# Layer 1 of an adapter and feed-forward kernel: the middle tap of the convolution added by accumulating DMAs

## The chip, the cores and the metric

The kernel runs on 1 core of one Trainium2 chip. The metric is device time in microseconds, the median of several runs. The engines are PE (TensorE, matrix multiplies and transposes), DVE (VectorE), ACT (ScalarE), POOL (GpSimd) and SP (SyncE, which here issues DMAs only).

## The reference

`x` is 8 batches of 512 tokens of 256 numbers. Two layers are applied, each `x = x + ffn(cond(x))`. Layer 0 is an adapter with a layer norm, and a feed-forward block with ternary weights and activations quantized per token. Layer 1, the one that is changed:

```python
def _L1_ffn_ref(x, w1, conv_w, conv_b, w2):
    h = bit_linear(x, w1)                       # 256 -> 1024, ternary weights
    h = depthwise_conv1d(h.transpose(0, 2, 1), conv_w, conv_b)   # 3 taps along the 512 tokens, padding 1
    h = h.transpose(0, 2, 1)
    h = jax.nn.silu(h)
    return bit_linear(h, w2)                    # 1024 -> 256
```

`bit_linear` quantizes each token's row by its largest absolute value to 8 bits.

## The kernel before, in words

All is one program with instruction lists written out by hand for each engine. Each engine runs its list in order; semaphores hold it where it needs another's result. The lists are: an opening, a loop `slot1` over batches of layer 0, a closing in which both layers overlap, and a loop `slot2` over rounds `s` of layer 1. In a round, several batches stand in the pipeline at once: `x` and the linear layer of batch `s`, the first product and the convolution of batch `s-1`, the silu and second product of batches `s-2` and `s-3`.

The 1024 hidden channels of a batch lie as 8 blocks `f` of 128 partitions with 512 tokens along each. For each block:

- PE makes the product into a PSUM bank (`up`, L1337), and DVE dequantizes it into `apad` (`dequant`, L1018);
- ACT writes the last tap into the bank (`last_tap`, L608), and DVE adds the first tap to it and writes `conv[b % 2]`, which is half of `raw_all` (`first_tap`, L1025, it counts up `p_first`);
- POOL writes the middle tap and the bias into `mid` (`middle_tap`, L805, it counts up `p_mid`). For every two blocks, a quarter `q` of the batch, POOL adds `mid` onto `conv` (`tap_sum`, L812, 128 x 1024 f32, it counts up `p_sum`). There are two `mid` buffers, so `middle_tap` waits for the sum two quarters back.

When all four quarters are there, PE transposes them, 128 tokens `k` at a time (`transpose_conv(b, k)`, L1350). ACT applies silu (L617) into one of two buffers `g2`. DVE takes the largest absolute value of each token (`absmax2`, L1031), and then a scale and its reciprocal; ACT rounds to 16-bit codes (`round2`, L627); SP issues a DMA transpose (`transpose2`, L399), and PE multiplies by the second weights (`down2`, L1365). DVE adds the result to `x` (`final2`, L1049), and SP stores it (L403). Of the same round are `load2` on SP (L389, 256 KB of weights of the linear layer), `spread_of_up` (L790) and `round_y` (L784) on POOL, and `scale_of_down` (L795) on POOL.

PE's order in a round puts `transpose_conv(s-2, 0)` after `up(s-1, 4)`; ACT's puts `silu(s-2, 0)` between the last taps of blocks 3 and 4; DVE's puts `absmax2(s-2, 0)` before `first_tap(s-1, 4)`.

Of the kernel before, what the change touches and what calls it, by code (L numbers as in the profile page):

```python
# [6 lines left out]
ALU = mybir.AluOpType  # L7
# [4 lines left out]
BF16 = mybir.dt.bfloat16  # L12
# [3 lines left out]
P = 128  # L16
# [12 lines left out]
def build_program(nc, t):  # L29
    B, S, D = t["x"].shape  # L30
    H = t["w1a"].shape[1]
# [5 lines left out]
    TB = S // P  # L37
# [4 lines left out]
    with ExitStack() as ctx:  # L42
        def sb(name, shape, dt=F32):
            return ctx.enter_context(nc.sbuf_tensor(name, shape, dt))

        def sem(name):
            return ctx.enter_context(nc.semaphore(name))

        def sems(name, n):
            return [sem(f"{name}{k}") for k in range(n)]  # L50

        def wait(eng, s, n):

            if isinstance(n, int) and n <= 0:
                return
            eng.wait_ge(s, n)
# [3 lines left out]
        def bank(k, n=1):  # L60
            return psum[:, k, :] if n == 1 else psum[:, k:k + n, :]
# [25 lines left out]
        taps = sb("taps", [P, KH, 3])  # L87
# [13 lines left out]
        gam = [sb(f"gam{k}", [P, D]) for k in range(2)]  # L101
        bet = [sb(f"bet{k}", [P, D]) for k in range(2)]
        dqb = [sb(f"dqb{k}", [P, S]) for k in range(2)]
        mid_all = [sb(f"mid{k}", [P, 2 * S + 1]) for k in range(2)]
        hT = sb("hT", [A + 1, S])
        xx = [sb("xx", [P, 2, D]), dqb[0][:, :].rearrange("p (a d) -> p a d", a=2)]

# [28 lines left out]

        xs = sb("xs", [P, PAIRS, 2, D])

        lowb = mid_all[0][:, 0:H].bitcast(BF16)
        junk = mid_all[1][:, 0:H].bitcast(BF16)  # L140
        BANK_AD, BANK_DN, BANK_QT, BANK_UP, BANK_IN = 0, 1, 2, 3, 7

        BANK_TOTAL = [BANK_UP + 3, BANK_UP + 3, BANK_IN, BANK_IN]
# [77 lines left out]
        apad = sb("apad", [P, KH, SP2])  # L221
# [6 lines left out]
        qs2 = [sb(f"qs2_{k}", [P, 1]) for k in range(2)]  # L228
        dq2 = [sb(f"dq2_{k}", [P, 1]) for k in range(TB)]

        mid = [mid_all[k][:, 1:2 * S + 1].rearrange("p (r s) -> p r s", r=2) for k in range(2)]
        BANK_C, BANK_D2 = 5, 1


# [32 lines left out]
        p_last = sem("p_last")  # L267
        p_mid = sem("p_mid")
        p_first = sem("p_first")
        p_sum = sem("p_sum")  # L270
        p_cT = sems("p_cT", TB)
        p_silu = sems("p_silu", TB)
        p_am2 = sem("p_am2")
# [29 lines left out]
        def tile(b, j):  # L303
            return TB * b + j + 1
# [373 lines left out]
        def _(pool):  # L678
# [119 lines left out]
            def middle_tap(b, f):  # L798
                pool.wait_ge(p_a, KH * b + f + 1)
                if b == 0:  # L800
                    pool.wait_ge(s_const, 32)
                    pool.wait_ge(s_tern[3], 1)
                    pool.wait_ge(s_wsum, 4)
                wait(pool, p_sum, TB * b + f // 2 - 1)
                pool.tensor_scalar(mid[f // 2 % 2][:, f % 2, :], apad[:, f, 1:S + 1], taps[:, f, 1:2],  # L805
                                   convb[:, f:f + 1], ALU.mult, ALU.add).then_inc(p_mid, 1)

            def tap_sum(b, q):
                c = conv[b % 2]
                pool.wait_ge(p_first, KH * b + 2 * q + 2)  # L810
                pool.wait_ge(p_mid, KH * b + 2 * q + 2)
                pool.tensor_tensor(c[:, 2 * q:2 * q + 2, :], c[:, 2 * q:2 * q + 2, :],  # L812
                                   mid[q % 2][:, :, :], ALU.add).then_inc(p_sum, 1)

            def round2(b, k):
                pool.wait_ge(p_qs2[k], b + 1)
# [28 lines left out]
            def slot2(s):  # L845
                on(middle_tap, s - 1, 0)
                on(middle_tap, s - 1, 1)
                on(middle_tap, s - 1, 2)
                on(scale_of_down, s - 3, 1)
                on(scale_of_down, s - 3, 2)  # L850
                on(tap_sum, s - 1, 0)
                on(middle_tap, s - 1, 3)
                on(scale_of_down, s - 3, 3)
                on(middle_tap, s - 1, 4)
                on(tap_sum, s - 1, 1)
                on(spread_of_up, s)
                on(round_y, s, 1)
                on(round_y, s, 0)
                on(scale_of_down, s - 2, 0)
                on(middle_tap, s - 1, 5)  # L860
                on(middle_tap, s - 1, 6)
                on(middle_tap, s - 1, 7)
                on(tap_sum, s - 1, 2)
                on(tap_sum, s - 1, 3)
# [293 lines left out]
        def _(pe):  # L1158
# [181 lines left out]

            def transpose_conv(b, k):
                if k == 0:
                    pe.wait_ge(p_sum, TB * b + TB)
                    if b == 0:
                        pe.wait_ge(s_gelu, tile(B - 1, TB - 1))
                    wait(pe, p_silu[TB - 1], b)
                else:
                    pe.wait_ge(p_silu[k - 1], b + 1)
                for f in range(KH):
                    ins = pe.transpose(bank(BANK_C + f // KT)[:, (f % KT) * P:(f % KT + 1) * P],  # L1350
                                       conv[b % 2][:, f, k * P:(k + 1) * P], id32[:, :])
                ins.then_inc(p_cT[k], 1)
# [16 lines left out]
            def slot2(s):  # L1369
                on(transpose_conv, s - 3, 3)  # L1370
                on(transpose_x, s, 0)
                on(up, s - 1, 0)
                on(up, s - 1, 1)
                on(up, s - 1, 2)
                on(down2, s - 3, 0)
                on(linear, s, 0)
                on(transpose_x, s, 1)
                on(up, s - 1, 3)
                on(up, s - 1, 4)
                on(transpose_conv, s - 2, 0)  # L1380
                on(linear, s, 1)
                on(down2, s - 3, 1)
                on(transpose_conv, s - 2, 1)
                on(up, s - 1, 5)
                on(up, s - 1, 6)
                on(up, s - 1, 7)
                on(down2, s - 3, 2)
                on(transpose_conv, s - 2, 2)
                on(spread_scales, s)
                on(transpose_y, s)  # L1390
                on(down2, s - 3, 3)
# [67 lines left out]
```

## Time and profile before

| | us |
|---|---|
| median of 3 runs | 321.74 |
| lowest and highest | 318.56, 323.08 |
| span of the profiled execution | 319.6 |

The profiled execution is one run of the program; its span reaches from the first to the last instruction, and no other time of that execution is given. Busy shares of it: DVE 87%, PE 83%, POOL 81%, ACT 75%. Layer 0 fills the first 140 us or so, layer 1 the time from about 160 us on. Busy times of one engine can overlap a little where one instruction starts before the one in front has ended, so a group's mean is slightly longer than its share of the engine's time.

### The profile page before, as it was taken

The page shows a single profiled execution, that of the slowest core. Times are in us where ns is not written, and L with a number is a line of the kernel's source. Part 1 is how long each engine was busy: PE and PEld are TensorE (multiplying, and loading weights), DVE is VectorE, ACT ScalarE, POOL GpSimd, SP SyncE. Part 2 cuts the span into 40 slices and gives each one's busy share as a digit, 9 for nine tenths or more (in the row PEclk, how much of TensorE's full clock was granted, in tenths as well). Part 3 has the DMA queues.
Part 4 walks back from the last instruction along what each step waited for, and adds up shares of the span by engine and source line. Part 5 has one row for each costly group of instructions (what it writes and reads, how often), then busy time and mean ns, then how long its engine had stood idle before and what let it go on. Part 6 is the DMA issues. An engine that isn't in the chain of part 4 may idle for free. (4 is left out here: it accounts for less than half of the span.)

```text
span 319.6 us, 6460 instructions
## 1 busy us (share of the span) xinstructions
PE 264.5 (83%) x1676; PEld 179.7 (56%) x1700; DVE 276.6 (87%) x606; ACT 240.6 (75%) x366; POOL 259.2 (81%) x402
## 2 busy tenths in 40 slices
PE   6679878869798887999889797989899898967574
PEld 6234334535455454566656665868587686745452
DVE  0778988896899989955899999999999999999671
ACT  4588897966776487567566888889989888978770
POOL 2567899996898988759999999998989799898310
PEclk9977799999999999999999999999999999999997
DMA  7995773579496368454430333445436373444764
GB/s 249 320 363 118 222 197 76 113 159 213 100 215 126 75 87 178 69 100 91 44 66 2 60 74 66 118 98 91 111 93 122 70 98 82 101 98 100 120 145 115
DMA packets 90745, 39.50 MB, mean 124 GB/s; under 512 B 73005, under 2 KB 88141, under 8 KB 90710
## 3 DMA queue, kind: packets, MB, share of 16 engines
q1 hardware_dynamic: 84532, 30.47, 46.8%
q10 hardware_dynamic: 6178, 8.62, 8.6%
q8 instruction: 14, 0.23, 0.3%
q14 instruction: 21, 0.17, 0.2%
HBM read 18.11 MB, written 4.19 MB: 70 GB/s over the span
## 5 line engine op out<-in xcount | busy, mean ns | idle before, releaser
L812 POOL TENSOR_TENSOR raw_all<-raw_all,mid 128x1024 f32<-128x1024 f32 x32 | 63.7, 2000 | 0.7 <-DVE raw_all L1025 0.7
L548 ACT ACTIVATE g<-banks,dqz 128x1024 f32<-128x1024 f32 x32 | 35.5, 1112 | 24.4 <-POOL r L757 21.2
L805 POOL TENSOR_SCALAR mid<-apad,taps,convb 128x512 f32<-128x512 f32 x64 | 48.8, 774 | 0.5 <-DVE apad L1018 0.5
L608 ACT ACTIVATE banks<-apad,taps 128x512 f32<-128x512 f32 x64 | 42.3, 682 | 6.9 <-DVE apad L1018 6.8
L970 DVE TENSOR_REDUCE am<-g 128x1 f32<-128x1024 f32 x32 | 38.6, 1211 | 8.6 <-ACT g L548 8.5
L1025 DVE SCALAR_TENSOR_TENSOR raw_all<-apad,taps,banks 128x512 f32<-128x512 f32 x64 | 45.8, 743 | 0.0
L1018 DVE TENSOR_TENSOR apad<-banks,dqb 128x512 f32<-128x512 f32 x64 | 40.9, 684 | 4.6 <-PE banks L1337 4.5
L757 POOL TENSOR_SCALAR r<-g,qs 128x1024 uint16<-128x1024 f32 x32 | 36.8, 1153 | 6.2 <-DVE qs L982 5.9
L1365 PE MATMUL banks<-tern,q1T 128*128 128x256 bf16 x256 | 33.8, 276 | 9.5 <-DMA q1T<-r 8.0
L1227 PE MATMUL banks<-tern,qT 128*128 128x512 bf16 x117 | 36.6, 388 | 5.5 <-ACT qcT L540 3.3
L627 ACT ACTIVATE r<-g,qs 128x1024 uint16<-128x1024 f32 x32 | 36.6, 1144 | 5.3 <-DVE qs L1044 3.2
L1298 PE MATMUL banks<-wl,x2T 128*128 128x256 f32 x128 | 33.0, 387 | 8.8 <-ACT x2T L577 6.8
L1031 DVE TENSOR_REDUCE am<-g 128x1 f32<-128x1024 f32 x32 | 38.8, 1213 | 1.2 <-ACT g L617 1.2
L1241 PE MATMUL banks<-tern,q1T 128*128 128x256 bf16 x256 | 33.2, 272 | 5.7 <-DVE xs L989 4.1
L1350 PE MATMUL banks<-id,raw_all 128*128 128x128 f32 x256 | 33.5, 274 | 3.6 <-ACT g L617 2.5
L617 ACT ACTIVATE g<-banks 128x1024 f32<-128x1024 f32 x32 | 32.5, 1014 | 4.0 <-PE banks L1350 3.7
L1365 PEld LDWEIGHTS banks<-tern,q1T 128*128 128x128 f16 x256 | 23.8, 98 | 18.5 <-DMA q1T<-r 12.5
L1337 PE MATMUL banks<-yT,tern 128*128 128x512 bf16 x115 | 29.7, 379 | 3.9 <-DVE raw_all L1025 2.4
L1241 PEld LDWEIGHTS banks<-tern,q1T 128*128 128x128 f16 x256 | 24.1, 97 | 15.7 <-issue 6.7
L1350 PEld LDWEIGHTS banks<-id,raw_all 128*128 128x128 f32 x256 | 28.9, 141 | 7.1 <-ACT g L617 3.9
L1298 PEld LDWEIGHTS banks<-wl,x2T 128*128 128x128 f32 x128 | 21.8, 190 | 15.1 <-issue 11.2
L1228 PE MATMUL banks<-bias9b,qcT 128*128 128x512 bf16 x64 | 24.8, 387 | 0.0
(116 smaller groups left out, 561.5 us busy)
## 6 DMA issues: line engine op xcount, KB each, us to landing
out_y<-xs SPq DMA_DIRECT2D x32, 128.0 KB, 2.0
xs<-in_x ACTq DMA_DIRECT2D x7, 512.0 KB, 5.7
x2T<-in_xT ACTq DMA_DIRECT2D x4, 512.0 KB, 5.2
wl<-in_cwl SPq DMA_DIRECT2D x8, 256.0 KB, 2.7
xT<-in_xT ACTq DMA_DIRECT2D x3, 512.0 KB, 4.2
raw_all<-in_w1a ACTq DMA_DIRECT2D x1, 1024.0 KB, 5.0
cw<-in_cw SPq DMA_DIRECT2D x16, 64.0 KB, 5.0
gam<-in_gamma SPq DMA_DIRECT2D x8, 128.0 KB, 3.0
```

The lines of the kernel that those rows point to most:

```text
L608: act.activation(bank(BANK_U[g % 3]), apad[:, f, 2:S + 2], ACT.Copy, scale=taps[:, f, 2:3]).then_inc(p_last, 1)
L757: pool.tensor_scalar(r1[j][:, :], g1[j % 2][:, :], qs1[j % 2][:, 0:1], CODE, ALU.mult, ALU.add) \
L805: pool.tensor_scalar(mid[f // 2 % 2][:, f % 2, :], apad[:, f, 1:S + 1], taps[:, f, 1:2], convb[:, f:f + 1], ALU.mult, ALU.add).then_inc(p_ ...
L812: pool.tensor_tensor(c[:, 2 * q:2 * q + 2, :], c[:, 2 * q:2 * q + 2, :], mid[q % 2][:, :, :], ALU.add).then_inc(p_sum, 1)
L970: dve.tensor_reduce(am1[j % 2][:, :], g1[j % 2][:, :], AX_X, ALU.max, apply_absolute_value=True) \
L1018: dve.tensor_tensor(apad[:, f, 1:S + 1], bank(BANK_U[(KH * b + f) % 3]), dqb[b % 2][:, :], ALU.mult) \
L1025: dve.scalar_tensor_tensor(out=conv[b % 2][:, f, :], in0=apad[:, f, 0:S], scalar=taps[:, f, 0:1], in1=bank(BANK_U[(KH * b + f) % 3]), op0= ...
L1031: dve.tensor_reduce(am2[k % 2][:, :], g2[k % 2][:, :], AX_X, ALU.max, apply_absolute_value=True) \
L1241: pe.matmul(o, q1T[j][:, c, :].bitcast(F16), w_dn0[:, c, :], start=(c == 0), stop=False)
L1298: pe.matmul(bank(bank_y(b))[:, a * D:(a + 1) * D], x2T[:, 2 * k + a, j, :], wl1[par][:, j, :], start=(j == 0), stop=False)
L1350: ins = pe.transpose(bank(BANK_C + f // KT)[:, (f % KT) * P:(f % KT + 1) * P], conv[b % 2][:, f, k * P:(k + 1) * P], id32[:, :])
L1365: pe.matmul(o, q2T[k % 2][:, f, :].bitcast(F16), w_dn1[:, f, :], start=(f == 0), stop=False)
```

## The change

POOL's addition becomes a DMA that POOL issues: it reads `mid[q]` and adds it in the destination, `conv`. There are four `mid` buffers, one for each quarter, and four semaphores in place of one, which count 16 for each DMA. The buffers are no longer shifted by one element. The two scratch tiles `lowb` and `junk` of the opening lie in the new buffers.

```diff
-        mid_all = [sb(f"mid{k}", [P, 2 * S + 1]) for k in range(2)]
+        mid = [sb(f"mid{k}", [P, 2, S]) for k in range(TB)]
...
-        mid = [mid_all[k][:, 1:2 * S + 1].rearrange("p (r s) -> p r s", r=2) for k in range(2)]
...
-        p_sum = sem("p_sum")
+        p_sum = sems("p_sum", TB)
...
-                wait(pool, p_sum, TB * b + f // 2 - 1)
-                pool.tensor_scalar(mid[f // 2 % 2][:, f % 2, :], apad[:, f, 1:S + 1], taps[:, f, 1:2],
+                wait(pool, p_sum[f // 2], 16 * b)
+                pool.tensor_scalar(mid[f // 2][:, f % 2, :], apad[:, f, 1:S + 1], taps[:, f, 1:2],
                                    convb[:, f:f + 1], ALU.mult, ALU.add).then_inc(p_mid, 1)
...
             def tap_sum(b, q):
                 c = conv[b % 2]
                 pool.wait_ge(p_first, KH * b + 2 * q + 2)
                 pool.wait_ge(p_mid, KH * b + 2 * q + 2)
-                pool.tensor_tensor(c[:, 2 * q:2 * q + 2, :], c[:, 2 * q:2 * q + 2, :],
-                                   mid[q % 2][:, :, :], ALU.add).then_inc(p_sum, 1)
+                pool.dma_start(c[:, 2 * q:2 * q + 2, :].rearrange("p r s -> p (r s)"),
+                               mid[q][:, :, :].rearrange("p r s -> p (r s)"), accum_op=ALU.add) \
+                    .then_inc(p_sum[q], 16)
...
             def transpose_conv(b, k):
                 if k == 0:
-                    pe.wait_ge(p_sum, TB * b + TB)
+                    for q in range(TB):
+                        pe.wait_ge(p_sum[q], 16 * (b + 1))
```

The order of the lists stays. On POOL, in a round of the loop, the end of one batch and the start of the next stand like this before, with the semaphores that each waits for:

```order
L805 TENSOR_SCALAR mid<-apad,taps,convb 128x512 [waits p_sum,p_a] x3
L812 TENSOR_TENSOR raw_all<-raw_all,mid 128x1024 [waits p_mid,p_first] x2
L805 TENSOR_SCALAR mid<-apad,taps,convb 128x512 [waits p_sum,p_a] x3
L795 TENSOR_SCALAR dq_1<-s_1,ws 128x1 [waits p_s2,p_o1]
L795 TENSOR_SCALAR dq_2<-s_0,ws 128x1 [waits p_s2,p_o2]
```

And on POOL now, in the same place:

```order
L804 TENSOR_SCALAR mid<-apad,taps,convb 128x512 [waits p_sum2,p_a]
L804 TENSOR_SCALAR mid<-apad,taps,convb 128x512 [waits p_sum3,p_a] x2
L811 DMA raw_all<-mid 128x1024 [waits p_mid,p_first] x2
L804 TENSOR_SCALAR mid<-apad,taps,convb 128x512 [waits p_sum0,p_a] x2
L804 TENSOR_SCALAR mid<-apad,taps,convb 128x512 [waits p_sum1,p_a]
```

The additions of quarters 2 and 3 have become two DMAs in their place, and each middle tap waits for the DMA of its own quarter of the batch before.

## Rows read from the trace of the kernel before

**Rows 1.** The page: its first line, busy times, and busy tenths in 40 slices.

```profile
span 319.6 us, 6460 instructions
PE 264.5 (83%) x1676; PEld 179.7 (56%) x1700; DVE 276.6 (87%) x606; ACT 240.6 (75%) x366; POOL 259.2 (81%) x402
...
DVE  0778988896899989955899999999999999999671
```

**Rows 2.** Windows, three rounds: busy us of each engine, PEclk, DMA share, GB/s.

```profile
229.20:247.60 18.40, 16.74 (x124) 13.28 (x125) 18.32 (x36) 16.58 (x23) 16.87 (x22) 1.00 0.51 101
247.60:266.10 18.50, 17.05 (x126) 13.52 (x127) 18.39 (x36) 16.46 (x23) 16.72 (x22) 1.00 0.51 87
266.10:284.50 18.40, 14.51 (x108) 11.08 (x109) 18.32 (x36) 15.97 (x22) 17.29 (x24) 1.00 0.39 86
```

**Rows 3.** Waits, 157 to 300 us: us in total, times, longest.

```profile
POOL dqy L790 <- DVE sy L1006: 5.3, 7, 1.2
...
DVE apad L1018 <- PE banks L1337: 1.2, 3, 0.7
...
DVE xs L989 <- PE banks L1242: 0.3, 1, 0.3
...
DVE am L1031 <- ACT g L617: 0.2, 1, 0.2
```

**Rows 4.** Groups by line, 157 to 300 us: busy us, mean ns, idle before.

```profile
L812 POOL TENSOR_TENSOR raw_all<-raw_all,mid 128x1024 f32<-128x1024 f32 x32 | 63.7, 2000 | 0.7 <-DVE raw_all L1025 0.7
L805 POOL TENSOR_SCALAR mid<-apad,taps,convb 128x512 f32<-128x512 f32 x62 | 47.3, 774 | 0.5 <-DVE apad L1018 0.5
L1025 DVE SCALAR_TENSOR_TENSOR raw_all<-apad,taps,banks 128x512 f32<-128x512 f32 x64 | 45.8, 743 | 0.0
...
L1018 DVE TENSOR_TENSOR apad<-banks,dqb 128x512 f32<-128x512 f32 x61 | 38.9, 684 | 1.4 <-PE banks L1337 1.2
L1031 DVE TENSOR_REDUCE am<-g 128x1 f32<-128x1024 f32 x28 | 34.0, 1213 | 0.2 <-ACT g L617 0.2
```

**Rows 5.** Timeline of POOL in one round: start us, us, instruction, idle before.

```profile
236.06 0.27 POOL L790 TENSOR_SCALAR dqy<-sy,ws 128x4 f32<-128x4 f32 x1 [1.25 <-DVE sy L1006]
...
240.93 3.96 POOL L812 TENSOR_TENSOR raw_all<-raw_all,mid 128x1024 f32<-128x1024 f32 x2
```

**Rows 6.** Timelines of DVE, PE and ACT in the same round.

```profile
241.26 0.75 DVE L1025 SCALAR_TENSOR_TENSOR raw_all<-apad,taps,banks 128x512 f32<-128x512 f32 x1
...
250.83 1.21 DVE L1031 TENSOR_REDUCE am<-g 128x1 f32<-128x1024 f32 x1
...
247.56 1.04 PE L1350 MATMUL banks<-id,raw_all 128*128 128x128 f32 x8
...
255.00 1.04 PE L1365 MATMUL banks<-tern,q1T 128*128 128x256 bf16 x8
...
257.74 1.04 PE L1365 MATMUL banks<-tern,q1T 128*128 128x256 bf16 x8
...
249.54 1.01 ACT L617 ACTIVATE g<-banks 128x1024 f32<-128x1024 f32 x1
```

**Rows 7.** Timeline of SP's queue in the same round; the us are the issue's.

```profile
242.37 0.41 SPq L389 DMA_DIRECT2D wl<-in_cwl  x1
243.60 1.25 SPq L399 DMA_TRANSPOSE q1T<-r  x1
244.90 0.57 SPq L403 DMA_DIRECT2D out_y<-xs  x1
248.09 1.25 SPq L399 DMA_TRANSPOSE q1T<-r  x1
...
253.72 1.23 SPq L399 DMA_TRANSPOSE q1T<-r  x1
```

**Rows 8.** DMA: rates in 40 slices of 242.3:245.5, of 247.8:251.8; landing, 157 to 300.

```profile
GB/s 301 282 288 241 20 6 0 0 0 0 0 0 0 0 102 205 205 115 26 38 77 166 346 397 384 358 320 256 218 64 0 74 195 224 214 237 202 224 202 202
...
GB/s 0 0 0 0 0 0 0 0 0 0 0 0 0 0 26 156 225 215 205 230 202 202 220 212 202 182 202 331 374 369 287 92 0 0 0 0 0 0 0 0
...
q1T<-r SPq DMA_TRANSPOSE x29, 3.1
```

**Rows 9.** Timeline of the tail, 295 to 304 us.

```profile
295.78 2.00 POOL L812 TENSOR_TENSOR raw_all<-raw_all,mid 128x1024 f32<-128x1024 f32 x1 [0.71 <-DVE raw_all L1025]
...
297.83 1.09 PE L1350 MATMUL banks<-id,raw_all 128*128 128x128 f32 x8 [0.45 <-POOL raw_all L812]
...
298.96 1.02 ACT L617 ACTIVATE g<-banks 128x1024 f32<-128x1024 f32 x1 [0.17 <-PE banks L1350]
...
299.31 1.05 PE L1365 MATMUL banks<-tern,q1T 128*128 128x256 bf16 x8 [0.39 <-DMA q1T<-r]
...
300.01 1.22 DVE L1031 TENSOR_REDUCE am<-g 128x1 f32<-128x1024 f32 x1 [0.65 <-ACT g L617]
...
303.32 1.15 ACT L627 ACTIVATE r<-g,qs 128x1024 uint16<-128x1024 f32 x1 [0.92 <-DMA q1T<-r]
```

More of the change, by code:

```diff
@@ L137, in build_program @@
         xs = sb("xs", [P, PAIRS, 2, D])
-        lowb = mid_all[0][:, 0:H].bitcast(BF16)
-        junk = mid_all[1][:, 0:H].bitcast(BF16)
+        lowb = mid[0][:, :, :].rearrange("p r s -> p (r s)").bitcast(BF16)
+        junk = mid[1][:, :, :].rearrange("p r s -> p (r s)").bitcast(BF16)
         BANK_AD, BANK_DN, BANK_QT, BANK_UP, BANK_IN = 0, 1, 2, 3, 7
```

## The prediction

> **What bounds the kernel now.** I read the page first [rows 1]: DVE is busy 87% of the span, PE 83%, POOL 81%, and the tenths show DVE at 9 without a gap from the 23rd slice to the 37th, which is the second layer. The run shown in these rows has a span of 319.6 us; the median of the runs is 321.74 (318.56 to 323.08), so my sum is made against 319.6 and carried to the median by adding the same microseconds. Then the stretches [rows 2]: three successive rounds of the layer-1 loop, one batch each, take 18.4, 18.5 and 18.4 us (36 DVE instructions in each), and in each DVE is busy for 18.3 to 18.4 of them, POOL for 16.7 to 17.3. The DMA engines are about half used. So a round lasts as long as DVE's list of instructions; POOL has 1.1 to 1.8 us to spare per round. The waits from 157 to 300 us [rows 3] say the same from the other side: DVE's waits are 1.2 + 0.3 + 0.2 = 1.7 us in 143, while POOL waits for DVE (5.3 us). What POOL does is therefore not what a round's length is made of, provided that nobody gets POOL's product late.
>
> **What is removed.** Each `tap_sum` is one POOL addition of 2.00 us [rows 4], 32 in all, four per round, 8.0 us of POOL's round. They are replaced by 32 DMAs. Four `mid` buffers in place of two add no wait: a buffer is wanted again a round later, and a DMA that takes under 18 us is long over. The writes into `mid` now start at an even place; between 774 ns a piece for 512 columns [rows 4] and no change I cost this at nothing, since it lies in POOL's slack.
>
> The gain from POOL's freed time is small. DVE can only gain the 1.7 us that it waits [rows 3], and most of that is for matmuls; I take 0.5 us, bounds 0 and 1.7. The free time also does not start the following work earlier, because POOL's next item after the second sum waits for DVE's scale already (1.25 us idle at 236.06) [rows 5].
>
> **What the issue costs.** POOL spends something to issue a DMA; no row of before has one from POOL. The nearest are SP's, 0.57 us for a plain store and 1.25 us for a transpose [rows 7]. I take 1.0, ends 0.3 and 2.5. Up to 2.0 + 1.7/4 = 2.4 us per DMA it stays within POOL's own slack.
>
> **Where the product is wanted.** PE transposes the sum (`transpose_conv(b,0)`), and waits for all four quarters of batch b. In a steady round: DVE ends the last first tap, `first_tap(b,7)`, at 241.26 + 0.75 = 242.0 [rows 6]; POOL has ended both last sums at 240.93 + 3.96 = 244.9 [rows 5]; PE starts the transposes at 247.56 for 1.04 us; ACT's silu (1.01 us) starts at 249.54; DVE's `absmax2(b,0)` starts at 250.83 [rows 6]. In the tail, where nothing else stands between them, the three hand-overs take 0.03 to 0.05 us each [rows 9]. So the sum may land as late as 250.83 - 0.03 - 1.01 - 0.04 - 1.04 - 0.05 = 248.7 before DVE stands still; today there is 3.8 us in hand. Between 242.0 and 250.83 DVE works through its own list, so this allowance of 6.7 us from the last first tap is the same each round and does not grow when a round is longer. Any excess is paid in full by DVE, once per round.
>
> **How late the DMA lands.** Quarter 2 is issued when the last middle tap ends, 240.93 [rows 5]; a transpose issued at 248.09 has its first packets at about 249.3 [rows 7, 8], so quarter 2's data begins at about 242.0. Quarter 3 is issued from 242.0 on. In the same stretch the engines must carry SP's other transfers [rows 7]: the linear weights (issued 242.37), a transpose (243.60), a store (244.90). Prices: 256 KB of weights at the 397 GB/s seen in that stretch, 0.7; a 256 KB transpose at about 205 GB/s [rows 8], 1.3; a 128 KB store 0.4. The accumulating transfer of 512 KB is not in the trace. Lower end: a copy at the best rate seen, 0.524 MB at 397 GB/s, 1.3 us. Upper end: each byte of the sum is read from two places, both at the transpose's rate, 4.9 us. I take the rate of the nearest row, the transpose, which also reads and writes this core's memory: 0.524 MB at 205 to 215 GB/s, 2.5 us. From 242.0: 2.5 + 2.5 + 0.7 + 1.3 + 0.4 = 7.4, and 0.2 to the semaphore: 249.6, against 248.7 allowed. **Stall 0.9 to 1.0 us per round.** At 1.3 us each it would be 247.2, no stall; at 4.9 it would be 254.4, 5.7 per round.
>
> Of the other transfers, the transposes feed `down2`. The one issued at 248.09 shares the engines with quarter 0 (issued near 247.6) and can be 2.5 us late; its matmuls start at 255.00 [rows 6], some 3.8 after it landed. Quarter 1 follows `first_tap(b,3)`, near 251, and is over by 255; the transpose of 253.72, whose matmuls start at 257.74 [rows 6], lands after 3.1 us [rows 8], has about 0.9 us in hand and only grazes it. These I cost at nothing; with longer transfers they are the next to be late.
>
> The Trainium skill (page "DMA: Bandwidth & Descriptors", section "Anatomy of one DMA — SWDGE (gpsimd) path") gives a transfer issued from POOL about 2.0 us plus its bytes at 436 GB/s, an estimate of 3.2 us here; by it quarter 3 would land at 245.2 and the stall term of the sum would be 0. No row of before tests it, and it speaks of copies on idle engines. Its page "Collectives: The Full Stack" (section "The bandwidth ceiling: the fold count and why AG ≠ RS ≠ AR") says that a DMA that adds needs two source reads and delivers half as fast, about 31/2 GB/s per engine, an estimate of 2.1 us of data on 16 engines; by that the stall would be 0.1 to 0.2 us. That rule speaks against the change, though less than the row I took.
>
> **The tail.** Batch 7's last sum starts at 295.78 and ends at 297.78; PE's transposes wait for exactly that (0.45) [rows 9]. The DMA issued then has data at 296.9, shares with one transpose and lands near 300.7, 2.9 us later. `down2(6,1)` stands behind it on PE and goes from 299.31 to 301.8, and with it the transpose that waits for its bank; but the chain there already waits for other transposes, and `round2(7,0)` had 0.92 us of waiting for one [rows 9]. About half gets through: +1.5, ends 0 and 3.
>
> **Sum.** Rounds with batches 1 to 6 in them: 6 x 1.0 = 6.0; tail 1.5; POOL's relief -0.5: **+7.0 us**, 319.6 to 326.6 for the span, 321.7 to about **329** for the median.
>
> **The rivals.**
> 1. *Forecast, 0.48*: PE gets the sum up to 2 us late per round. Stall 0.4 to 2.0, so +3.5 to +14: 325 to 336.
> 2. *All hidden, 0.33*. The addition lands inside the 6.7 us allowed: transfers of 1.3 to 2.2 us. For it: 3.8 us in hand today, engines half idle [rows 2]. Against: the other transfers fall into just this stretch. It is also where the skill's first rule would lead. Stall 0, tail 0 to 3, relief 0.5: -1 to +3, 321 to 325. This ends on the other side of the forecast: not slower. It decides at a transfer of 2.0 us with my queue.
> 3. *The DMA engines become the bound, 0.13*. They are busy 0.51 x 18.4 = 9.4 us a round [rows 2]; four transfers of 4.9 add 19.6, together 29.0 against 18.4, +10.6 a round, +64 over six: 386; at 3.5 each 23.4, +5, 352. It decides above (18.4 - 9.4)/4 = 2.25 us each, so my own 2.5 stands at its edge. The same picture results if POOL's issue costs over 2.4 us.
> 4. *Faster by 2%, 0.06*. POOL's additions slow DVE's two-operand instructions. The first tap takes 743 ns, the dequantizing product 684 for the same columns [rows 4]; if the difference were POOL's doing, 64 x 0.06 = 3.8, with the 1.7 of waits 5.5: 316. Against: the medians do not spread.
>
> **How the numbers follow.** This kernel's runs spread 1.4%, and 2%, 6.4 us, is about what can be told from no change. Above 328.2 lie 0.29 of the forecast's 0.48 and all 0.13 of the third: slower 0.42. Within: 0.19 and the 0.33 of the second: 0.52. Faster 0.06. The range goes from 319 (below the hidden case) to 345 (a transfer of about 3 us); outside are most of the third case and the fourth.
>
> **What would show it.** DVE gets a wait before `absmax2` for ACT's silu, of about 1 us per round, with PE's first transposes waiting for a DMA; POOL's busy time falls by 63.7 us less what issuing shows; DVE's means of 684, 743 and 1213 ns stay; the DMA share of a round rises from 0.51 to 0.9 or more; rounds of 19.4 us. Wrong if the sum lands less than 6.7 us after the last first tap (then case 2), or if the SP transposes, 3.1 us today [rows 8], take over 5 and `final2` waits for matmuls too (case 3).

## The result, and the profile after

The change made the kernel slower: the median of 4 runs is 346.06 us (341.95 to 348.21), that of before beside them 321.59 (318.56 to 323.08). The ratio is 1.0738, 95% interval 1.0625 to 1.0852. Forecast were 329 us and a range that ended at 345. Here and below a median is that of all runs, and a ratio is that of the fast ones alone, without those that lie over 1.5% above a kernel's fastest (here 348.21), so it can differ a little from the quotient of the medians. The profiled execution has a span of 343.3 us, 23.7 more than before's 319.6.

The page after: its first lines, and the tenths of DVE and of the DMA engines.

```profile
span 343.3 us, 6468 instructions
...
PE 278.5 (81%) x1676; PEld 190.3 (55%) x1700; DVE 275.0 (80%) x606; ACT 240.9 (70%) x366; POOL 222.8 (65%) x402
...
DVE  0668987998899899659979879696997999976361
...
DMA  7992674867774574464997979989999998999864
```

DVE is as busy as before in microseconds (275.0 against 276.6), but its row of nines [rows 1] is broken from the middle on, and there the DMA row is nearly all nines. Windows of three rounds, from one `absmax_y` (L1000) to the next, and of the tail behind the last of them; the columns are those of [rows 2]:

```profile
200.92:222.70 21.78, 18.30 (x125) 14.60 (x125) 18.33 (x36) 16.53 (x23) 12.41 (x21) 0.92 0.95 175
...
222.70:244.61 21.91, 18.30 (x125) 14.30 (x126) 18.44 (x36) 16.81 (x23) 12.41 (x21) 0.92 0.99 176
244.61:264.89 20.28, 17.17 (x123) 13.17 (x124) 18.42 (x37) 16.62 (x23) 12.42 (x21) 1.00 1.05 183
...
285.33:343.30 57.97, 39.82 (x249) 30.05 (x249) 37.40 (x75) 33.07 (x37) 18.56 (x34) 0.82 0.87 156
```

A round lasts 20.3 to 21.9 us in place of 18.4, with DVE still busy for 18.4: it now stands still for 1.9 to 3.5 us in each. POOL is down from 16.8 to 12.4. The DMA share has gone from 0.51 to about 1. PE's granted clock was 0.92 in the first two of these rounds, and they lost more (2.8 and 3.4 us) than the two at 1.00 behind them (2.0 each). By the starts of L1000, the round that ends at 200.92 is 3.8 us longer than before's, the next ones 2.8, 3.4, 2.0 and 2.0, and the tail is 58.0 against 48.4: 14.0 us in the rounds, 9.5 in the tail, nothing ahead of them.

The waits of 157 to 325 us (us in total, times, longest), the two groups of POOL, and the DMA queues (packets, MB, share of 16 engines) of the same stretch:

```profile
ACT g L616 <- PE banks L1351: 17.6, 14, 4.2
...
DVE am L1031 <- ACT g L616: 13.5, 7, 4.4
...
PE banks L1351 <- DMA raw_all<-mid: 13.0, 6, 3.3
PE banks L1366 <- DMA q1T<-r: 11.4, 6, 3.4
```

```profile
L804 POOL TENSOR_SCALAR mid<-apad,taps,convb 128x512 f32<-128x512 f32 x62 | 47.8, 806 | 21.8 <-DVE apad L1018 21.8
L811 POOL DMA_DIRECT2D raw_all<-mid x32 | 27.6, 867 | 10.3 <-DVE raw_all L1025 9.7 <-POOL mid L804 0.2
```

```profile
q0 software_dynamic: 4608, 16.78, 55.7%
q1 hardware_dynamic: 35584, 12.20, 43.6%
```

Two kinds of wait have appeared side by side: PE for the sum (`raw_all<-mid`), which goes on to ACT and DVE, and PE for SP's transposes (`q1T<-r`). Before, DVE's wait for ACT's silu was 0.2 us [rows 3]. The adding DMAs are q0: 55.7% of 168 us, 93.6 us for 32, so **2.93 us of all 16 engines each**. From issue to landing they take 6.9 us in the median (4.5 at the least), the transposes 6.2 in place of 3.1 [rows 8].

One round as timelines of POOL, DVE, PE, ACT and DVE again (start us, us, instruction, idle before):

```profile
251.10 0.78 POOL L811 DMA_DIRECT2D raw_all<-mid  x1
252.52 0.85 POOL L811 DMA_DIRECT2D raw_all<-mid  x1 [0.65 <-DVE raw_all L1025]
...
251.47 0.75 DVE L1025 SCALAR_TENSOR_TENSOR raw_all<-apad,taps,banks 128x512 f32<-128x512 f32 x1
...
255.39 1.05 PE L1366 MATMUL banks<-tern,q1T 128*128 128x256 bf16 x8 [1.95 <-DMA q1T<-r]
...
260.62 1.06 PE L1351 MATMUL banks<-id,raw_all 128*128 128x128 f32 x8 [0.50 <-DMA raw_all<-mid]
...
261.72 1.02 ACT L616 ACTIVATE g<-banks 128x1024 f32<-128x1024 f32 x1 [0.58 <-PE banks L1351]
...
259.73 1.29 DVE L1018 TENSOR_TENSOR apad<-banks,dqb 128x512 f32<-128x512 f32 x2 [1.23 <-PE banks L1337]
...
262.78 1.22 DVE L1031 TENSOR_REDUCE am<-g 128x1 f32<-128x1024 f32 x1 [0.32 <-ACT g L616]
```

The last first tap ends at 252.22, quarter 3's DMA is issued at 252.52, and PE starts on the sum at 260.62: 8.4 us behind the first tap, where 6.7 to landing was allowed. PE also stood 1.95 us for a transpose at 255.39; what it does behind that is late, and DVE waits 1.23 us for an `up` product. So in this round DVE stands longer by way of the late transpose than by way of the late sum (0.32 us).

The chain of waits in the first of the windows above shows sum and clock together (start us, us, what):

```profile
208.85 8.55 DMA raw_all<-mid
...
217.64 1.94 PE banks L1351 x8
```

The 8 transposes of PE behind the sum took 1.94 us in place of 1.06. PE had stood 3.29 us for the sum, and its granted clock was 1.2 GHz (0.5) from 217.1 to 220.5 us.

### The profile page after: what moved, and what is told of

Read it like the earlier page. It is cut to its first block, busy times and chain, and to the rows that moved or that the text cites. A ratio compares the mean times of both kernels' runs of the same rounds, so it can differ in the third digit from the quotient of the medians.

```text
span 343.3 us, 6468 instructions
## 1 busy us (share of the span) xinstructions
PE 278.5 (81%) x1676; PEld 190.3 (55%) x1700; DVE 275.0 (80%) x606; ACT 240.9 (70%) x366; POOL 222.8 (65%) x402
## 4 chain that ended last, share of the span: by engine, by line
DMA 24%; PE 21%; issue 18%; POOL 18%; DVE 10%; ACT 4%; SPq 3%; POOLq 0%; DVEq 0%; ACTq 0%
DMA q1T<-r 10%; DMA raw_all<-mid 10%; PE banks L1298 6%; POOL r L756 4%; PE banks L1366 3%; PE banks L1351 3%; POOL mid L804 3%; POOL xs L729 2%; DMA cw<-in_cw 2%; PE banks L1241 2%; PE banks L1227 2%; ACT r L626 2%; DMA bet<-in_beta 1%; SPq L334 1%; DVE zg L939 1%
## 5 line engine op out<-in xcount | busy, mean ns | idle before, releaser
L1366 PE MATMUL banks<-tern,q1T 128*128 128x256 bf16 x256 | 37.7, 297 | 15.2 <-DMA q1T<-r 14.6
L1351 PE MATMUL banks<-id,raw_all 128*128 128x128 f32 x256 | 38.8, 302 | 13.6 <-DMA raw_all<-mid 13.0
L1351 PEld LDWEIGHTS banks<-id,raw_all 128*128 128x128 f32 x256 | 33.2, 157 | 18.3 <-issue 15.6
L756 POOL TENSOR_SCALAR r<-g,qs 128x1024 uint16<-128x1024 f32 x32 | 37.5, 1174 | 6.8 <-DVE qs L982 6.5
L1366 PEld LDWEIGHTS banks<-tern,q1T 128*128 128x128 f16 x256 | 26.0, 106 | 25.7 <-DMA q1T<-r 18.6
L1298 PE MATMUL banks<-wl,x2T 128*128 128x256 f32 x128 | 35.7, 411 | 4.1 <-issue 3.8
L1241 PE MATMUL banks<-tern,q1T 128*128 128x256 bf16 x256 | 33.2, 272 | 6.6 <-DVE xs L989 6.0
L811 POOL DMA_DIRECT2D raw_all<-mid x32 | 27.6, 867 | 10.3 <-DVE raw_all L1025 9.7
L1241 PEld LDWEIGHTS banks<-tern,q1T 128*128 128x128 f16 x256 | 24.2, 97 | 15.9 <-issue 9.2
L1298 PEld LDWEIGHTS banks<-wl,x2T 128*128 128x128 f32 x128 | 23.6, 205 | 11.4 <-issue 7.3
L1049 DVE SCALAR_TENSOR_TENSOR xs<-banks,dq,xs 128x256 f32<-128x256 f32 x32 | 15.4, 481 | 11.8 <-PE banks L1367 11.7
```

Of the source, the lines that this page charges most:

```text
L756: pool.tensor_scalar(r1[j][:, :], g1[j % 2][:, :], qs1[j % 2][:, 0:1], CODE, ALU.mult, ALU.add) \
L1241: pe.matmul(o, q1T[j][:, c, :].bitcast(F16), w_dn0[:, c, :], start=(c == 0), stop=False)
L1298: pe.matmul(bank(bank_y(b))[:, a * D:(a + 1) * D], x2T[:, 2 * k + a, j, :], wl1[par][:, j, :], start=(j == 0), stop=False)
L1366: pe.matmul(o, q2T[k % 2][:, f, :].bitcast(F16), w_dn1[:, f, :], start=(f == 0), stop=False)
```

## The experiments

All ratios are to the kernel before, on the same chip; the brackets hold the 95% interval. S stands for the theory that the sum lands too late, T for the one that traffic makes SP's transposes late.

**The traffic without the wait for the sum.**

```diff
-                pool.dma_start(conv quarter q, mid[q], accum_op=ALU.add).then_inc(p_sum[q], 16)
+                pool.dma_start(mid[q], conv quarter q, accum_op=ALU.add).then_inc(p_sum[q], 16)
...
-                    for q in range(TB): pe.wait_ge(p_sum[q], 16 * (b + 1))
+                    pe.wait_ge(p_first, KH * (b + 1))
```

> The same 32 accumulating DMAs of 512 KB, issued by POOL at the same places, but in the other direction: conv is added onto mid, which nobody reads, and PE's first transpose waits for the first taps alone. The middle tap and the bias are left out of the result. Theory S (the time goes because PE waits for the sum, which lands 7 to 8 us after its issue): the waits before transpose_conv and silu go, 320 to 325 us. Theory T (the DMA engines are full, four transfers of 2.9 us and 9 us of others in a round of 18.4, and SP's transposes get late with everything behind them): nothing is gained by not waiting for the sum, 338 to 346 us, q1T still landing after about 6 us. Both in part: 326 to 337.

Measured 341.5 us, 1.0679 [1.0576, 1.0782]. Waits, 157 to 325 us:

```profile
PE banks L1365 <- DMA q1T<-r: 18.5, 10, 3.6
...
DVE xs L1049 <- PE banks L1366: 11.5, 8, 2.8
```

With no wait for a sum anywhere, 21 us of the loss are there, and PE's waits are for the transposes. "Transposes at nothing" is refuted.

**Two quarters by DMA, two by POOL**: first 2 and 3, then 0 and 1. The edit is the same in all kernels that mix (`BY_DMA` is the set):

```diff
+                if q in BY_DMA:
                     pool.dma_start(...)
+                else:
+                    pool.tensor_tensor(c[:, 2 * q:2 * q + 2, :], c[:, 2 * q:2 * q + 2, :],
+                                       mid[q][:, :, :], ALU.add).then_inc(p_sum[q], 1)
```

> Quarters 2 and 3 of each batch are added by DMAs, quarters 0 and 1 by POOL as before. The DMA load of a round is about 9.2 + 2 x 2.9 = 15 us of 18.4, but the two DMAs that PE waits for next keep their places. S: quarter 3 still lands 7 us or more after its issue, a stall of 0.5 to 2 us per round and the tail's loss remain, 328 to 338 us. T: the engines are no longer full, 321 to 326 us.

> Quarters 0 and 1 by DMA, 2 and 3 by POOL. The load is the same as with quarters 2 and 3, but these two DMAs are issued half a round before PE wants them. S and T both: 320 to 325 us, no wait of PE for raw_all<-mid. If this one is over 328 while quarters 2 and 3 by DMA are not, it is the transposes of SP that share the engines with quarters 0 and 1 that cost the time.

Quarters 2 and 3: 339.56 us, 1.059 [1.0506, 1.0673], just above what S allowed. Quarters 0 and 1: 332.04 us, 1.0261 [1.0139, 1.0383], where I had expected 320 to 325. With half the load, the pair that must land in the short stretch costs more than twice as much as the pair with time in hand; with 2 and 3 the wait for the sum (`PE banks L1357 <- DMA raw_all<-mid`) is 16.0 us, with 0 and 1 there is none, and the waits are for transposes. These are not late by an average load, though. In the trace of quarters 0 and 1 (an execution of 333.18 us; the others took 326.15 to 335.66) two transposes took over 10 us to land, this one and one issued at 294.40:

```profile
248.74 10.23 DMA q1T<-r
```

What happened there is taken apart below, with quarter 0 alone.

**The DMAs almost without bytes**: of each quarter only 16 of 1024 columns are added, the rest of the middle tap is left out.

```diff
-                pool.dma_start(conv quarter q, mid[q], accum_op=ALU.add)
+                pool.dma_start(c[:, 2 * q, 0:16], mid[q][:, 0, 0:16], accum_op=ALU.add)
```

> All 32 DMAs at their places and with their waits, but each adds 16 columns of one block (8 KB) in place of 1024 columns (512 KB); the rest of the middle tap is left out of the result. It keeps POOL's issue (0.87 us) and the fixed part of the landing, and takes the bytes away. S and T both: landing in 2 to 3 us, inside the 6.7 us allowed, 318 to 322 us. If it stays over 328 us, it is the issue or the fixed latency and not the bytes. Under 315 us it would show a gain from POOL's freed time.

Measured 321.86 us, 1.0071 [1.002, 1.0121]. Windows of two rounds:

```profile
195.47:213.79 18.32, 16.93 (x126) 13.46 (x125) 18.23 (x35) 16.43 (x23) 12.46 (x21) 1.00 0.49 103
213.79:232.29 18.50, 17.13 (x126) 13.39 (x125) 18.33 (x36) 16.45 (x23) 12.47 (x21) 1.00 0.57 102
```

The rounds are those of before, with POOL at 12.5 us and 32 issues of 866 ns. So the issue, the fixed part of the landing and POOL's freed time together come to 0.7%, at most 1.2, and nearly the whole loss hangs on the bytes.

**Quarter 3 alone, and a control** in which POOL adds all four quarters in the new buffers.

> Only quarter 3, the last one that PE waits for, is added by a DMA. The queue that I now take for the cause: two additions of 2.9 us each, the linear weights, a transpose and a store all fall between the last first tap and the 6.7 us that DVE allows. With quarter 2 back on POOL (its sum ends about 1 us after the last first tap) one addition is left: 2.9 + 0.7 + 1.3 + 0.4 + 1.1 before the data = 6.4 us at most, landing in 5 to 6.5 us, a stall of 0 to 0.3 per round. 320 to 326 us. If instead any addition by DMA in this place costs a stall (a fixed latency over 6.7 us), 330 us or more.

> All four quarters by POOL again, with the four buffers, the four semaphores and the aligned places of the change: the control for everything but the DMA. POOL's addition took 2.34 us with aligned buffers in the mixed kernels, against 2.00 before, 1.4 us of POOL per round in which it had 1.1 to 1.8 to spare. Theories S and T both: 320 to 325 us. Over 328 us would mean that part of the loss in the mixed kernels is this one.

Quarter 3 alone: 336.42 us, 1.0453 [1.0369, 1.0537], a miss (320 to 326 expected). The control: 326.66 us, 1.0212 [1.0144, 1.0279], also above what was expected, with these groups:

```profile
L818 POOL TENSOR_TENSOR raw_all<-raw_all,mid 128x1024 f32<-128x1024 f32 x32 | 75.3, 2364 | 0.0
...
L1012 DVE TENSOR_SCALAR sy<-amy 128x4 f32<-128x4 f32 x7 | 7.4, 1058 | 0.3
```

The unshifted `mid` makes POOL's own addition 2.36 us in place of 2.00 [rows 4], 32 of them 11.6 us. The longer additions aren't the whole reason for the 2%: DVE's small instruction `sy` (a scale, 0.17 us where nothing disturbs it) takes 7.4 us in its seven rounds, and before it took 3.0:

```profile
L1006 DVE TENSOR_SCALAR sy<-amy 128x4 f32<-128x4 f32 x7 | 3.0, 433 | 0.3
```

That is 4.4 us more of DVE's time, on the engine that sets the round, where the spans of the two traces lie 2.6 us apart (322.2 and 319.6); what happens to `sy` comes with the held-back DMA below. The control for kernels in which POOL adds most quarters is this one, not before.

One DMA a round, of 2.9 us, costs far more than its share. In the trace (an execution of 338.45 us, the fastest took 332.73) a single DMA is much of it: issued 0.04 us behind a transpose, it took 8.5 us in packets and 10.80 to land, and its round 25.3 us:

```profile
268.40 10.80 DMA raw_all<-mid
```

Without it the loss isn't nothing: three other rounds of that trace took 18.4, 18.8 and 20.7 us.

**More packets for the same bytes**: rows of 1 KB in place of 4 KB.

```diff
-        mid = [sb(f"mid{k}", [P, 2, S]) for k in range(TB)]
+        mid_all = [sb(f"mid{k}", [P, 4, S // 2 + 8]) for k in range(TB)]
+        mid = [m[:, :, 0:S // 2] for m in mid_all]
```

> The changed kernel with mid stored in pieces of 256 columns with a gap of 8 between them, so that each partition's row of a DMA is four pieces of 1 KB and not one of 4 KB; as many DMAs and bytes. If SP's transposes are late because their small packets take turns with packets of 4 KB that hold an engine for 0.33 us each, they land in 4 to 5 us in place of 5.7, and the time falls to 330 to 340 us. If it is the bytes alone, landings stay and the time is 342 to 350; more packets may also make POOL's issue dearer than 0.87 us (over 2 us each would bind POOL and give more than 350).

Measured 361.41 us, 1.1269 [1.1191, 1.1346], above both theories (330 to 340 and 342 to 350), and POOL's issue, 1.29 us, is within its slack. The engines' time for one DMA rises to 3.66 us and its landing to 8.7. All 32 transposes land after 5.4 us in the median, in the change after 5.7: shorter packets hardly helped them. The time follows what the engines have to do.

**Batch 7's sums by POOL**, all others by DMA.

```diff
+                if b == B - 1:
+                    pool.tensor_tensor(conv quarter, conv quarter, mid[q], ALU.add).then_inc(p_fin, 1)
+                    return
```

> The changed kernel, but batch 7, the last one, is added by POOL. The tail after the last batch's scale (L1000) took 58.0 us against 48.5 before, 9.5 of the 23.7 lost, where I had reckoned 1.5. If the last batch's own DMAs (late sum, and batch 6's transposes beside them) make that, the tail falls to about 49 to 51 us and the total to 336 to 339 us. If the tail is long because of what came before it, it stays over 56 us and the total at 343 or more.

Measured 338.04 us, 1.0542 [1.0463, 1.0621]: 8 us less than the change in the medians, 6 by the ratios, and its tail is 50.5 us in place of 58.0.

**No DMA transposes in layer 1**: plain copies of the same tiles in their place, in before and in the change; the quantized tokens then lie untransposed, which leaves the second product meaningless.

```diff
-                sp.dma_start_transpose(q2T[k % 2][:, :, :], r2[k % 2][:, :]).then_inc(p_q2T[k], 16)
+                sp.dma_start(q2T[k % 2][:, :, :].rearrange("p f s -> p (f s)"), r2[k % 2][:, :]).then_inc(p_q2T[k], 16)
```

> The kernel before with layer 1's 32 DMA transposes replaced by plain copies of the same 256 KB, so that the transposition is left out of the result; a control for the next one. A copy lands in about 2.7 us where a transpose takes 3.1; DVE bounds the rounds either way: 318 to 323 us.

> The changed kernel with the same plain copies for layer 1's transposes (the transposition is left out of the result). Theory B (bytes: four additions of 2.9 us and the rest fill the engines): the copies carry the same bytes, the round's load stays near 20 us, 335 to 346 us. Theory X (an adding DMA and a DMA transpose that are in flight together slow each other beyond their bytes; in the kernel with quarter 3 alone on a DMA the engines moved about 100 GB/s while both ran, and each alone runs at 180 to 200 or more): most of the loss goes, 322 to 332 us, sums landing in about 5 us and copies in 3 to 4.

Before without transposes: 318.81 us, 0.9928 [0.9881, 0.9975]. The change without them: 335.96 us, 1.0462 [1.0364, 1.056]. The 17.2 us between the two are the change's loss with the transposes out of play, and there PE waits for the sum (8 times, up to 4.4 us), while the copies that stand for transposes hold PE for 1.5 us in all. DVE stands 1.0 to 2.3 us before `absmax2` in five rounds, and 5.4 in the tail. So S alone gives 17 us, T alone (the first experiment) 21, both together 24.5: they overlap, as they would if a round that is already stretched by the one gave time to the other. The copies carry the same bytes, so this run doesn't take their load away.

**A copy in place of the addition**: `mid` is copied over `conv`, so the first and last taps are lost.

> The changed kernel with the 32 DMAs as plain copies of mid over conv, without the addition (the two other taps are left out of the result): what the adding costs in the DMA. An adding packet of 4 KB takes 0.33 us, so that a DMA fills the engines for 2.9 us; a copy of one read should take half, 0.16 and 1.4 us. B: load 5.6 + 9 = 15 us of 18.4, landing 3 to 4 us, 320 to 327 us. X, if it is any 4 KB packet beside a transpose and not the addition: still over 330 us.

Measured 326.16 us, 1.0206 [1.0106, 1.0305]. The q0 rows of 157 to 325 us:

```profile
q0 software_dynamic: 4608, 16.78, 28.1%
...
raw_all<-mid POOLq DMA_DIRECT2D x32, 512.0 KB, 3.3
```

28.1% of 168 us over 32 is 1.48 us of the engines each. Adding takes 2.93 for the same bytes, 1.98 times as long. By the ratios, some 70% of the loss (0.0738 less 0.0206) is the price of adding.

**Quarter 0 alone.** It has more time to land than the others and loads the engines little.

> Only quarter 0 by DMA, the one that PE wants half a round later, and beside it only the transpose that has 3.8 us in hand. The control without DMAs is at 326.7 (its POOL additions take 2.36 us in place of 2.00); POOL gets 1.5 us of relief per round here. B and X both: 321 to 328 us, no waits for raw_all<-mid. Above 330 us there would be a cost of a single adding DMA that neither theory has.

Measured 337.0 us, 1.0446 [1.0323, 1.0569]. That is a clear miss: neither S nor an average load explains it. Windows of three rounds:

```profile
217.00:238.87 21.87, 17.14 (x126) 13.38 (x125) 18.51 (x37) 16.46 (x23) 17.52 (x22) 1.00 0.76 133
238.87:257.13 18.26, 17.11 (x126) 13.38 (x125) 18.18 (x36) 16.43 (x23) 16.04 (x21) 1.00 0.71 104
257.13:281.77 24.64, 19.69 (x126) 15.65 (x125) 18.80 (x37) 16.52 (x23) 17.68 (x22) 0.86 0.73 106
```

Good rounds and very bad ones alternate. In the last one PE's granted clock fell too (0.86, and PE was busy for 19.7 us in place of 17.1), so its 6.2 us too many aren't all the wait. What the bad ones have in common is when two DMAs are issued; SP's and POOL's timelines and what follows on PE:

```profile
212.39 1.25 SPq L400 DMA_TRANSPOSE q1T<-r  x1
...
212.56 0.68 POOL L814 DMA_DIRECT2D raw_all<-mid  x1
...
222.25 0.94 PE L1372 MATMUL banks<-tern,q1T 128*128 128x256 bf16 x7 [2.77 <-DMA q1T<-r]
...
252.56 1.25 SPq L400 DMA_TRANSPOSE q1T<-r  x1
...
252.73 0.66 POOL L814 DMA_DIRECT2D raw_all<-mid  x1
```

Both times POOL issues 0.17 us after SP. The chain of waits (start us, us, what) then goes through that transpose, which lands in 3.1 us normally:

```profile
212.39 9.82 DMA q1T<-r
...
252.56 10.55 DMA q1T<-r
```

The rates of 211 to 223 us, in slices of 0.3 us, say that the two don't simply share the bandwidth:

```profile
GB/s 222 0 0 0 0 0 0 0 41 166 191 176 149 164 147 106 104 43 28 15 28 43 6 79 73 72 72 109 171 224 213 186 196 153 55 230 189 305 230 59
```

After 2 us at 150 to 190 the traffic sinks to between 6 and 43 GB/s for 2 us with both transfers unfinished. The packet records show the pair: the adding DMA's first packet comes 0.8 to 0.9 us behind the transpose's first; then 15 to 17 of its 128 packets of 4 KB take over 2 us (0.33 in the median), and for some 2 us few of the transpose's packets start; most of its packets are as short as ever (18 ns in the median). The adding DMA lasts 7.1 to 7.8 us in packets (3.0 alone), the transpose 5.7 to 5.9 (1.4 alone). It happened 3 times in 8. Three runs take this meeting apart.

**Quarter 0 held back, quarter 0 issued one instruction later, quarter 0 as a copy.**

```diff
+                    if b >= 2:
+                        pool.wait_ge(p_q2T[2], 16 * (b - 1))
                     pool.dma_start(...)
```

```diff
-                on(tap_sum, s - 1, 0)
                 on(middle_tap, s - 1, 3)
+                on(tap_sum, s - 1, 0)
```

> One adding DMA for each batch, that of quarter 0, the other three quarters by POOL; here POOL issues it only once the transpose of tokens 2 of the batch two before has landed. With quarter 0 alone and no such wait the kernel took 337.0 us, with two long rounds (21.9 and 24.6 us), and in these the adding DMA had begun 0.8 to 0.9 us after that transpose and lasted 7 to 8 us in place of 3, the transpose 5.7 to 5.9 in place of 1.4. Theory X (the long rounds come from an adding DMA that begins inside a transpose): no such meeting is left, no adding DMA lasts over 5 us in packets, the rounds are back near 18.4 us, and the time falls to 323 to 330 us; POOL's own wait, up to 4 us in a round, is taken from its idle time. Rival (the long rounds have another cause, and the meetings follow from it): the time stays at 333 us or above and long rounds are still there.

> The same one adding DMA for each batch with no added wait: it is issued one instruction later in POOL's list, behind the middle tap of block 3, so that it begins 0.7 to 2.6 us later against the transpose of tokens 2. Theory X: the meetings at 0.8 to 0.9 us behind the start of a transpose are gone or rare, 322 to 330 us. Rival: 333 us or above. If the new place only meets the next transpose, tokens 3, X expects that transpose at 4 to 6 us in packets and the time in between.

> The same one DMA for each batch at the same place as with quarter 0 alone, as a plain copy of mid over conv: quarter 0 lacks its first and last tap, nothing else is left out. If the addition in the destination is what makes the meeting with a transpose long: no DMA of this kind over 4 us in packets and no transpose over 4, time 321 to 328 us. If any large DMA from POOL's queue that begins inside a transpose does it, long rounds appear and the time is 332 us or above.

*One instruction later*: 320.07 us, 0.9996 [0.9956, 1.0037]. **All of the 4.5% is gone**, with the same DMAs, bytes and packets. Windows of two rounds, and the two issues, now 1.60 us apart:

```profile
215.47:233.96 18.49, 16.84 (x124) 13.40 (x125) 18.32 (x37) 16.44 (x23) 16.93 (x22) 1.00 0.64 129
233.96:252.22 18.26, 16.75 (x124) 13.38 (x125) 18.18 (x36) 16.43 (x23) 16.90 (x22) 1.00 0.68 131
```

```profile
210.86 1.25 SPq L400 DMA_TRANSPOSE q1T<-r  x1
...
212.46 0.88 POOL L814 DMA_DIRECT2D raw_all<-mid  x1
```

No adding DMA but the first lasts over 3.0 us in packets. *Held back by a wait*: 336.05 us, 1.0493 [1.039, 1.0597]. The meetings are gone there too (all adding DMAs but the first, 4.4, last 3.0 to 3.2), yet the time was not won, a second miss: my expectation took POOL's wait to be free. Timelines of POOL and DVE in a round:

```profile
237.08 0.90 POOL L816 DMA_DIRECT2D raw_all<-mid  x1 [3.43 <-DMA q1T<-r]
...
239.45 2.59 POOL L820 TENSOR_TENSOR raw_all<-raw_all,mid 128x1024 f32<-128x1024 f32 x1
...
239.31 2.77 DVE L1014 TENSOR_SCALAR sy<-amy 128x4 f32<-128x4 f32 x1
```

POOL stands 3.1 to 4.1 us, its next addition slips on to `sy`, the small DVE instruction that takes 0.17 us elsewhere, and that one takes 2.7 to 2.8 us, in every such round (20.8 to 21.0 us). Over seven rounds `sy` takes 14.5 us, with the DMA one instruction later 2.2: 12.3 of the 16.0 us between these two traces. Of this below. *As a copy*: 323.09 us, 1.0085 [1.0035, 1.0135]. The meetings come about (3 of 8, the copy 5.0 to 5.5 us in packets in place of 1.4, the transpose 4.3 to 5.4), so the addition is not needed for them; they cost less, and the copy is over sooner. My stated price for that case, 332 us or above, was too high.

**The whole change with the same move, and the moved kernel with shifted buffers.**

> The whole change, four adding DMAs for each batch, with that of quarter 0 issued one instruction later, behind the middle tap of block 3. With quarter 0 alone this move gave all of its 4.5% back. Theory X+S (both a meeting of adding DMAs and transposes, and sums and transposes late by the load of four DMAs of 2.9 us): only the meeting of quarter 0 is moved, the other three DMAs still fill the engines, 336 to 346 us. If the one place of quarter 0 is most of the loss of the whole change too: 322 to 332 us.

> One adding DMA for each batch, that of quarter 0, issued behind the middle tap of block 3 (this was level with the kernel before), and the mid buffers again shifted by one element as before. Expected: POOL's additions of the other quarters take 2.00 us in place of 2.36; POOL is not what the rounds wait for, so 317 to 322 us, same. If POOL's time did count in that kernel: 314 to 317 us, faster than both.

The change moved: 343.99 us, 1.0745 [1.0672, 1.0819], no different from the change. Its trace, like the change's own, has no adding DMA over 4.5 us in packets: the bad meeting is not what the whole change suffers from. It is in the traces of quarter 0, of quarters 0 and 1, and of quarter 3 alone. Shifted: 320.52 us, 0.9994 [0.9952, 1.0036]; POOL's additions are back at 2.06 us and it brings nothing. No version that computes the whole result beat the kernel before.

## Why the prediction was wrong

The direction and the mechanism of the forecast (the sum lands late, PE, ACT and DVE pass the wait on) are right; the size is not. The step that failed is **"These I cost at nothing"**, said of SP's transposes: alone they cost 21 us. Beside it the sum's own stall was mis-sized: 6.0 in the rounds and 1.5 in the tail were forecast, and with the transposes out of play it cost 17.2.

- *POOL's relief, -0.5*: none seen. With the bytes gone and POOL just as relieved the kernel stood at 1.0071.
- *The issue, 1.0 us*: 0.87, in POOL's slack, free. Right.
- *The adding transfer, 2.5 us* (ends 1.3 and 4.9): 2.93 of the engines, which also moves the landing of two in a row by 0.9 us. It is the mis-sized term of the sum's stall. The price was taken from a transpose; the copy of the same bytes takes 1.48, and adding twice that. The rule that a DMA that adds reads two sources and delivers half as fast (the Trainium skill, "Collectives: The Full Stack", section "The bandwidth ceiling: the fold count and why AG ≠ RS ≠ AR") agrees in its ratio: 1.98 was measured. The 2.1 us estimated from its figure is too low.
- *Landing 7.6 us behind the last first tap, 6.7 allowed*: in the round shown PE had the sum 8.4 behind it. That is 1.7 over what was allowed, where 0.9 to 1.0 was said. DVE did not pay it in the one place that the forecast named: it stood 0.32 us before `absmax2`, 1.23 for the `up` product and 0.23 for `y`, 1.8 together, by which the round is longer than DVE's work. With the transposes out of play it paid 1.0 to 2.3 before `absmax2`. The rule of about 2.0 us plus the bytes at 436 GB/s (the Trainium skill, "DMA: Bandwidth & Descriptors", section "Anatomy of one DMA — SWDGE (gpsimd) path"), an estimate of 3.2 us from issue to landing, was met by no adding DMA: 4.5 at the least, 6.9 in the median. The plain copies took 3.3 in the median.
- *Transposes at nothing*: they land after 6.2 us in place of 3.1. Alone they give 21 us, where both together give 24.5. The price was in the prediction: it gave the third of these transposes 0.9 us in hand, and a single adding DMA ahead of it takes 2.9. A transpose whose first packet falls 0.3 us behind an adding DMA's takes 3.8 to 4.7 us in packets (1.4 alone), nine times in the change's trace.
- *Tail +1.5* (0 to 3): +9.5. There the chain is transpose, product, transpose, with nothing to cover any of it: it holds transposes for 7.52 and 8.14 us. Batch 7's sums by POOL shorten the tail by 7.4 us. PE's granted clock is 0.82 in the tail against before's 0.96, and these are groups of 8 matmuls behind such waits, which take 1.04 us at 2.4 GHz and here 1.72 and 1.94, at 1.2 GHz for most of it:

```profile
312.42 1.72 PE L1366 MATMUL banks<-tern,q1T 128*128 128x256 bf16 x8 [3.43 <-DMA q1T<-r]
...
320.38 1.94 PE L1351 MATMUL banks<-id,raw_all 128*128 128x128 f32 x8 [2.81 <-DMA raw_all<-mid]
```

  How much of the 9.5 is the clock isn't separated by a run. As an estimate: on the chain of the tail stand six such groups of 1.49 to 1.95 us, 10.5 us in all, where six at 2.4 GHz take 6.2; before's tail had one, of 1.61. So up to 3.7 us of it. The forecast had no term for the clock, in the tail or in the rounds.
- *Third rival, engines as the bound, 0.13*: it named its own threshold, 2.25 us each, and the forecast's own 2.5 stood above it. At 2.93 it reads 4 x 2.93 + 9.4 = 21.1 against 18.4, +2.7 a round; the rounds gained 2.0 to 3.8 and the share of the engines went to 0.95 to 1.15. The sign that the prediction gave for this case, transposes over 5 us, came too. This rival came nearest to the picture, and had been priced only for transfers of 3.5 and 4.9. It isn't all of it: with quarters 2 and 3 alone by DMA the same sum reads 15.3 of 18.4, and 5.9% were lost.

What stays open: the parts overlap, so no sum of S and T is exact; how many bad meetings there were in the executions that were not profiled isn't known; and why a transpose and another DMA hold each other up was seen and moved away, not explained.

## What to carry to other kernels

Moving work from an engine to DMAs is paid in the DMA engines' time: add what each transfer takes of them to what they do already, per round, and compare with the round's length before looking at any landing time; an accumulating DMA counted twice its copy here. Ask then which small, latency-bound transfers share the engines with it: here their landing doubled. And the place of a DMA's issue against a DMA transpose can be worth more than its bytes: look in the trace for transfers that last several times their usual length, see what was issued just ahead of them, and move one by an instruction, with an order and not with a wait. And before moving an engine's work to the DMA queues, look for short instructions of another engine that it lengthens: here POOL's additions, slipped on to DVE's `sy`, cost 12 us.

## What the runs showed of the hardware

- An adding DMA of 512 KB within on-chip memory takes 2.93 us of 16 engines, its 4 KB packets 0.33 us; the copy takes 1.48 us, its packets 0.16 (the change and its copy). With 1 KB rows adding takes 3.66 us, and POOL's issue 1.29 us in place of 0.87; a copy's issue takes 0.57.
- An adding DMA from POOL that is issued 0.16 to 0.18 us behind a DMA transpose from SP lasts 6.7 to 7.8 us in packets and the transpose 5.7 to 7.1, in all five cases in the traces of quarter 0 and of quarters 0 and 1. Three copies, issued 0.19 to 0.21 behind, lasted 5.0 to 5.5, and their transposes 4.3 to 5.4. At 0.04 us one adding DMA lasted 8.5 and another 3.9; at 0.10, 0.14, 0.34 and 0.50 us, in three other kernels, they lasted 3.3 to 3.6. So the distance of the issues alone doesn't decide it. Issued 1.6 us behind, neither is touched.
- POOL's addition of two 128 x 1024 f32 operands takes 2.00 us with one operand shifted by one element and 2.36 without the shift.
- DVE's 128 x 4 `sy` instruction stood from 239.31 to 242.08 while POOL's addition ran from 239.45 to 242.04, and so in each of the five rounds in which they met there (2.2 to 2.8 us for 0.17). In the control `sy` took up to 2.73 us, in the kernel before up to 1.28. The Trainium skill ("SBUF — State Buffer", section "SBUF: two separate sides") says that one of the two can block the other for a whole instruction, by a port pair that they share. The trace agrees in the length, `sy` ends 0.04 us behind POOL's addition; the page gives the pair to whichever starts first, and here `sy` shows the earlier start, by 0.14 us, and yet was the one that waited. No run here tests the ports.
